# One core, talking-heads attention with a routed feed-forward: the exponential of a tile's first half moves ahead of the copies of turned chunks, and the output bank is copied by ScalarE and added by GpSimd

## What is computed

```
q, k = rope(q), rope(k)                                # after x @ Wqkv.T + bqkv
logits = einsum('bhid,bhjd->bhij', q, k) * 16**-0.5
logits = einsum('bhij,gh->bgij', logits, Wpre)
attn = softmax(logits, axis=-1)
attn = einsum('bhij,gh->bgij', attn, Wpost)
out = einsum('bhij,bhjd->bhid', attn, v)               # then @ Wout.T + bout
x = layernorm(x + out)
```

## Time and profile before

| | us |
|---|---|
| median of 3 runs | 8371.17 (8367.39 to 8371.35) |
| the profiled execution | 8358.64 |
| its span | 8356.8 |
| TensorE busy | 7996.8 (96%) |
| VectorE busy | 7605.1 (91%) |
| ScalarE busy | 6848.0 (82%) |
| GpSimd busy | 6046.9 (72%) |

### The profile page before, as it was taken

The page is one execution under the profiler, slowest core; times in us unless marked ns, Lnnn a source line. Parts: engine busy times, 40 slices in busy tenths (PEclk is TensorE's granted clock), DMA queues, the critical chain, the costliest instruction groups (busy, mean ns, idle before and its releaser), DMA issues.

```text
span 8356.8 us, 449859 instructions
## 1 busy us (share of the span) xinstructions
PE 7996.8 (96%) x182764; PEld 4649.9 (56%) x182764; DVE 7605.1 (91%) x13390; ACT 6848.0 (82%) x11648; POOL 6046.9 (72%) x12006
## 2 busy tenths in 40 slices
PE   7999999998899999999889999999979999999997
PEld 4555555555555555555545555555554555555554
DVE  7999999997899999999789999999978999999996
ACT  5888888886688888888568888888857888888884
POOL 6777777774677777777477777777737777777773
PEclk9999999998999999999899999999989999999998
DMA  1011111112101111111211111111121011011112
GB/s 53 23 28 27 26 26 27 26 27 91 34 24 27 27 26 26 27 28 26 89 35 25 26 27 26 27 26 27 26 88 36 25 26 28 25 27 26 27 26 93
DMA packets 265756, 284.04 MB, mean 34 GB/s; under 512 B 41089, under 2 KB 252673, under 8 KB 261377
## 3 DMA queue, kind: packets, MB, share of 16 engines
q1 hardware_dynamic: 263680, 255.07, 11.3%
HBM read 78.75 MB, written 39.85 MB: 14 GB/s over the span
## 4 chain that ended last, share of the span: by engine, by line
PE 73%; DVE 12%; issue 10%; POOL 1%; ACT 1%; DVEq 1%; DMA 0%; SPq 0%; POOLq 0%; ACTq 0%
PE psS L1248 47%; PE psP L1267 15%; PE psO L1282 6%; DVE big L878 5%; DVE pl L906 2%; DVE spare L867 2%; PE psM L1293 1%; ACT big L694 1%; DVE ot L889 1%; PE psS L1378 1%; PE psM L1308 1%; PE psS L1407 1%; PE psS L1209 0%; DVE nb L867 0%; PE psS L1196 0%
## 5 line engine op out<-in xcount | busy, mean ns | idle before, releaser
L1248 PE MATMUL psS<-KH,AX 64*128 64x512 f16 x32768 | 3928.4, 377 | 52.0 <-DMA AX<-AX 50.1
L694 ACT ACTIVATE big<-psP 128x512 f16<-128x512 f32 x4096 | 2222.4, 595 | 826.2 <-PE psP L1267 822.9
L878 DVE SCALAR_TENSOR_TENSOR big<-psP,big 128x512 f16<-128x512 f32 x4096 | 2613.9, 679 | 175.5 <-ACT big L694 174.0
L675 ACT ACTIVATE pr<-psS,nb 128x1024 f32<-128x1024 f32 x2048 | 2289.7, 1118 | 192.9 <-DVE nb L867 190.1
L1248 PEld LDWEIGHTS psS<-KH,AX 64*128 64x128 f16 x32768 | 1451.5, 95 | 1513.5 <-DMA AX<-AX 51.7
L704 ACT ACTIVATE ph<-pr 128x1024 f16<-128x1024 f32 x2048 | 2166.8, 1058 | 32.3
L1248 PE MATMUL psS<-KL,AX 64*128 64x512 f16 x16384 | 2106.3, 377 | 0.0
L906 DVE TENSOR_TENSOR pl<-pr,ph 128x1024 f16<-128x1024 f32 (+1 forms) x2048 | 2078.3, 1015 | 0.0
L1267 PE MATMUL psP<-rh,ph 64*128 64x64 f16 x32768 | 1671.7, 191 | 131.4 <-DVE big L878 112.0
L1267 PEld LDWEIGHTS psP<-rh,ph 64*128 64x128 f16 x32768 | 1468.7, 95 | 557.9 <-DVE big L878 395.9
L1267 PE MATMUL psP<-rl,ph 64*128 64x64 f16 x32768 | 1667.0, 191 | 4.7 <-issue 4.3
(11 more groups left out here) (137 smaller groups left out, 6286.4 us busy)
## 6 DMA issues: line engine op xcount, KB each, us to landing
AX<-AX SPq DMA_DIRECT2D x2048, 64.0 KB, 2.0
ph<-in_xT SPq DMA_DIRECT2D x16, 512.0 KB, 8.7
xr<-in_x SPq DMA_DIRECT2D x64, 128.0 KB, 2.3
Q<-in_w SPq DMA_DIRECT2D x8, 1024.0 KB, 7.2
out<-V SPq DMA_DIRECT2D x16, 512.0 KB, 3.7
d_x<-x SPq DMA_DIRECT2D x60, 128.0 KB, 2.0
d_xn<-xn SPq DMA_DIRECT2D x60, 128.0 KB, 2.0
d_lg<-lg SPq DMA_DIRECT2D x60, 128.0 KB, 2.0
```

The costliest lines, as they stand in the source:

```text
L675: a.activation(pr[:, p, h * N2:(h + 1) * N2], psS[:, 2 * h:2 * h + 2, :].rearrange("p c n -> p (c n)"), ACT.Exp, bias=nb[:, p, h:h + 1], s ...
L694: a.activation(PT[:, hf * JH:(hf + 1) * JH, :, 0, i0:i0 + HQ], psP[:, ih, :].rearrange("p (j g i) -> p j g i", j=JH, g=H), ACT.Copy, scale ...
L878: v.scalar_tensor_tensor(out=PT[:, js, :, 1, i0:i0 + HQ], in0=psP[:, ih, :].rearrange("p (j g i) -> p j g i", j=JH, g=H), scalar=MDROP, in ...
L1248: mm = pe.matmul(psS[:, 2 * hp + half, :], AX[rows, k8, kq, s_, :], K_[rows, kq, hp, :], start=n == 0, stop=n == len(steps) - 1, tile_posi ...
```

## The change

In ScalarE's `slot`, `exps(T, t, 0)` now stands ahead of the two `mixed_high(T-2)` of the first half. Before it stood behind them. The second half keeps its order. In slots 3 and 11, VectorE's two `out_copy` parts are gone (but for the last one of a batch, which stays). In their place ScalarE copies the whole bank `psO` into a new SBUF tile `oraw` (128x512), between its second pair of `mixed_high` and `exps(T, t, 1)`, and GpSimd adds the two halves of `oraw` into `ot`, behind its `low`. A new semaphore `s_or` carries the hand-over.

```diff
+                def out_sum(n, half, R):
+                    g.wait_ge(s_or, b * (NIT * 2 - 1) + n + 1)
+                    g.wait_ge(s_y, R + 1)
+                    parts = oraw[:, :].rearrange("p (q s i) -> p q s i", q=GQ, s=2)
+                    apart(g)
+                    g.tensor_tensor(ot[:, :, half * GI:(half + 1) * GI],
+                                    parts[:, :, 0, :], parts[:, :, 1, :], ALU.add).then_inc(s_oc, 2)
...
                     if one:
                         low(T - 1, t_1, first and t < 3)
+                    if t % TG == 3 and not (first and t < TG) and it < NIT:
+                        out_sum(it * 2 + t // TG - 1, (t // TG + 1) % 2, b * NIT + it - (1 if t < TG else 0))
                     roots(it, t, 2)
...
+                def out_raw(n):
+                    Gd = b * (NIT * 2) + n
+                    a.wait_ge(s_F, (Gd + 1) * NC + NC)
+                    a.wait_ge(s_oc, Gd * 2 + 1)
+                    a.activation(oraw[:, :], psO[:, :], ACT.Copy).then_inc(s_or, 1)
...
+                    if live:
+                        exps(T, t, 0, early)
                     mixed(0)
                     mixed(1)
                     if live:
-                        exps(T, t, 0, early)
                         highs(T, t, 0, early)
...
                     mixed(2)
                     mixed(3)
+                    if t % TG == 3 and not (first and t < TG) and it < NIT:
+                        out_raw(it * 2 + t // TG - 1)
                     if live:
                         exps(T, t, 1, early)
...
-                def copied(it, t, first, part):
-                    if t % TG == 3 and not (first and t < TG) and it < NIT:
-                        out_copy((b * NIT + it) * 2 + t // TG - 1, (t // TG + 1) % 2, b * NIT + it - (1 if t < TG else 0),
-                                 part)
...
                         mixed_low(T - 2, t_2, 1)
-                    copied(it, t, first, 0)
                     rows(it, t, 1)
...
                         mixed_low(T - 2, t_2, 3)
-                    copied(it, t, first, 1)
```

More of the change, by code:

```diff
@@ L146, in seq_layer @@
         ot = sb("ot", [P, GQ, P])
+        oraw = sb("oraw", [P, GQ * P])
         xr = sb("xr", [P, DIM])
@@ L259, in seq_layer @@
         s_oc = sem("s_oc")
+        s_or = sem("s_or")
         s_xr = sem("s_xr")
```

## The result

The changed kernel takes 10158.52 us (median of 4 runs, 10149.33 to 10160.7), the kernel before 8369.51 us (4 runs, 8367.39 to 8371.35). The ratio is 1.2136 with a 95% interval of 1.2117 to 1.2155: 21% slower. The forecast was 10,075 us, 9,600 to 10,450.

The account below looks back on a forecast made before the run. VectorE's loop, with hole and collision, was the bound: 13 x 8.93 + 2 x 10.6 + 10.2 = 147.5 us a pass against 120.62; over 64 passes +1720, less 17, gives 10,075 us, range 9,600 to 10,450.

Parts of the forecast that it names:

- common slot: One of 13 in a pass, from first-half maximum to the next tile's: 8.93 us, against 6.58 before.
- The hole: VectorE idle between first-half maximum and chunk low parts, while ScalarE does exponential and copy: 1.78 us a slot.
- The collision: VectorE's 512-column `low` runs into GpSimd's `low`; next maximum starts at 5.38 us, without it 4.79; chance 0.60.
- The rival without it: VectorE's `low` passes beside GpSimd's: slot 8.34 us, total 9,700 us; chance 0.27, partial collision included.
- the two take turns: VectorE's and GpSimd's SBUF operations exclude each other, the later blocked; shared bandwidth would give a slot between 8.34 and 8.93.
- TensorE not the bound: TensorE's loop from scores through exponential and second turn to scores takes 8.2 us, under 8.93: some 0.7 us slack.
- Long slots: Slots 2 and 10, with output, take about 10.6 us each; slot 4, with output projection, 10.2 us.
- The output bank: Slots 3 and 11: VectorE loses 0.8 us of reductions, already counted in 8.93; the added copy and add cost 0.
- The clock: Rival: TensorE, idle about 2 of 9 us a slot, falls to half clock: about 15,700 us; chance 0.04.
- The 17 us taken off for the last tiles of a batch: In each batch's last seven tiles GpSimd mixes no queries and the collision goes: 28 x 0.6 = -17 us.
- The ground that the prediction gave against a falling clock: In a 17 us stretch of the earlier trace with TensorE 73% busy, the granted clock was 1.00.

Follow-up runs that it names:

- experiment 1: The changed kernel with the first half's exponential put back behind the two copies, leaving only the output bank's part: 8321.21 us, ratio 0.9942 to the kernel before.
- experiment 2: The kernel before with only the exponential moved ahead of the copies; VectorE keeps its output reductions: 10230.04 us, ratio 1.2216.
- experiment 4: The changed kernel with the first half's exponential between the two copies of turned chunks instead of ahead of both: 9250.74 us, ratio 1.1047.
- experiment 3: The changed kernel with VectorE's 512-column `low` moved behind the second half's maximum: 9813.05 us, ratio 1.1716.
- experiment 5: The changed kernel with VectorE's 512-column `low` moved ahead of the first pair of chunk low parts: 9666.94 us, ratio 1.1564.
- experiment 6: The changed kernel with 10 extra, overwritten score matmuls on TensorE in the second half of all slots but 2, 4 and 10: 10077.66 us, ratio 1.2057.

## Why the prediction was right

Step by step, in the order of the prediction, measured in the slot shown above (in us from the start of the first maximum):

| step | predicted | measured |
|---|---|---|
| exponential starts | 1.25 | 3031.87 - 3030.62 = 1.25 |
| first copy starts | 2.36 | 3032.98 - 3030.62 = 2.36 |
| chunk low part starts | 2.99 | 3033.60 - 3030.62 = 2.98 |
| GpSimd's `low` starts | 3.74 | 3034.34 - 3030.62 = 3.72 |
| VectorE's `low` starts | 4.18 | 3034.80 - 3030.62 = 4.18 |
| its duration | 1.25 | 1.25 |
| second maximum starts | 5.38 | 3035.97 - 3030.62 = 5.35 |
| common slot | 8.93 | 8.89 |

*The hole* is right in mechanism and size: 2.98 - 1.22 = 1.76 us, forecast 1.78. Experiments 1 and 2 put the whole loss on the exponential's place, and in experiment 4 a smaller hole loses less.

*The collision* is right: 0.57 us a slot, by experiment 3. The rival without it forecast a slot of 8.34, and experiment 3 is this case: 8.32. Its total was forecast at 9,700 and came out at 9,813; some 59 us of the difference are the clock, the rest is that the long slots were sized too short for it. That the two take turns is borne out too: the slot is 8.89, as near as can be to the 8.93 of that reading, and GpSimd's `low` kept its 1.16. In experiment 4, where VectorE starts first, GpSimd is the one that waits.

*TensorE not the bound* holds for the changed kernel. The value of its loop, 8.2 us, was an estimate with an allowance for hand-overs; experiment 5 shows that the next bound is a different loop, of 8.21 us, so that the number was near by accident.

*Long slots*: output slots were forecast at 10.6, slot 4 at 10.2. Between first-half maxima, slot 4 takes 10.05 in most passes. Slots 2 and 10 take mostly 10.26 and 10.27, and the slots ahead of them 9.29 and 9.13; the first piece of the output probably delays the next maximum. Two such slots together are 19.4 to 19.55, forecast 8.93 + 10.6 = 19.53.

*The output bank.* The forecast took its copy and its add to cost nothing, and that is right: slots 3 and 11 take 8.93 and 8.95 us on average, common ones 8.9. The gain of 0.8 us in each of these slots that it named is too large for both orders: 0.6 in the old one (experiment 1), 0.3 in the new one (experiment 2), where half of the reductions would have stood in time that the collision takes anyway.

*The clock* is the term that was missing from the sum. It was a rival priced as all or nothing, at 4 in 100. In fact it falls now and then, at some 92 us in all, and the forecast was 83 us too low (97 us for the profiled execution, 10,158.8 against 10,062). The rest agrees so well partly by luck: the long slots' errors, tenths of a us each way, happened to cancel, and so did smaller ones. The 17 us taken off for the last tiles of a batch are one of these: of the last seven slots of a batch's last pass only slots 13 and 14 fall below 8.9 us.

The ground that the prediction gave against a falling clock was also read wrongly. It took the earlier trace rows for a stretch in which TensorE is 73% busy at full clock. But that stretch, 2090 to 2107, is 12.4 us of unbroken work and 4.6 us of one wait, and right behind it the clock is at its lower level. TensorE's timeline in the kernel before:

```profile
2086.72 15.71 PE L1407 MATMUL psS<-big 128*128 128x256 f32 x64 [0.81 <-DVE big L1137]
2107.21 5.34 PE L1209 MATMUL psS<-ph,pl 128*128 128x512 f32 x8 [4.77 <-DVE ya L1167]
```

By stretch (stretch, us, TensorE busy, granted clock, DMA share, GB/s):

```profile
2107.20:2110.50 3.30, 3.29 (x4) 0.50 0.08 25
```

A mean over a stretch says little about a loop with a wait in every slot.

## What to carry to other kernels

When two full engines work a loop in strict order, an instruction moved ahead is priced by what it waits for, not by what it does: here the exponential waits for a maximum that the other engine has just ended, and everything put behind it becomes a hole in that engine. Follow the loop once around, instruction by instruction with starts from the trace; where it closes within one tile, no buffer or phase shift hides it. Then look at what the shifted phases now put side by side: a quarter of the slot's loss was two instructions that before seldom met. And a forecast that comes out can do so for another reason than the one given, as in experiment 2: look slot by slot before believing the sum.

## What the runs showed of the hardware

- TensorE's clock falls to its lower level (1.2 GHz) inside a steady loop in which nearly all waits are 2.0 us and shorter, but only in some tiles: in 47 of the 96 slots with a wait of 2.0 us and in 20 of the 452 with 1.9. This was not expected from the kernel before, whose stretches at that level all lay outside the tiles. With some 1.1 us of work put into these waits (experiment 6) 13 such falls are left in place of 68, all in the slot that got no added work. Filling the waits with work whose result is thrown away made the kernel 66 to 81 us faster. What decides which of two slots with the same wait sees a fall stays open.
- Of two subtractions with both inputs in SBUF, one on VectorE and one on GpSimd, the one that started second was held up and the first kept its time: VectorE's took 1.25 us in place of 0.68 behind GpSimd's (changed kernel), and GpSimd's took 1.61 in place of 1.16 behind VectorE's (experiment 4).
